# Leaf sweeps of a 64-node eigensolver: four small operations leave VectorE, three of them for ScalarE, and the order changes

## The reference, cut to what matters

```
def _L0_gnn_ref(features, A, W1, b1, W2, b2):
    deg = jnp.sum(A, axis=0) + jnp.sum(A, axis=1) - jnp.diagonal(A)
    d_inv_sqrt = jnp.where(deg > 0, jax.lax.rsqrt(deg), 0.0)
    L_norm = d_inv_sqrt[:, None] * (jnp.diag(deg) - A) * d_inv_sqrt[None, :]
    _, U = jnp.linalg.eigh(L_norm)
    agg = jnp.einsum('mn,bnd->bmd', U.T, features)
    h = jax.nn.relu(agg @ W1 + b1)
    return jnp.einsum('nm,bmd->bnd', U, h @ W2 + b2)
x = _layernorm(x + _L0_gnn_ref(x, adj, ...))   # layer 0: needs the eigenvectors
x = _layernorm(x + _L1_gnn_ref(x, adj, ...))   # layer 1: graph products, four LSTMs
x = _layernorm(x + _L2_gnn_ref(x, adj, ...))   # layer 2: products with batch norms
x = _layernorm(x + _L3_gnn_ref(x, adj, adj, ...))   # layer 3: masked attention
```

## Time and profile before

| what | value |
| --- | --- |
| median of 3 runs | 2172.83 us (2171.48 to 2173.25) |
| the profiled execution's own time | 2171.96 us |
| its span, first to last instruction | 2170.2 us |
| busy in the span: PE, PEld | 1808.6 us (83%), 1524.7 us (70%) |
| busy in the span: DVE, ACT, POOL | 1457.8 us (67%), 868.0 us (40%), 653.2 us (30%) |
| instructions | 31902 |

### The profile page before, as it was taken

The page is one execution under the profiler, slowest core; times in us unless marked ns, Lnnn a source line. Parts: engine busy times, 40 slices in busy tenths (PEclk is TensorE's granted clock), DMA queues, the critical chain, the costliest instruction groups (busy, mean ns, idle before and its releaser), DMA issues. The chain is left out here.

```text
span 2170.2 us, 31902 instructions
## 1 busy us (share of the span) xinstructions
PE 1808.6 (83%) x9508; PEld 1524.7 (70%) x9508; DVE 1457.8 (67%) x5806; ACT 868.0 (40%) x1784; POOL 653.2 (30%) x1040
## 2 busy tenths in 40 slices
PE   3454333326999999999999999999999998979997
PEld 2333333314988888888899999888887886857774
DVE  7999999985778555445444444444444777858886
ACT  2333222201344466333333333232332656646664
POOL 0001344402233466333323332413341113521111
PEclk9999766656999999999999999999999999989999
DMA  6000000000111000000000000000010412200111
GB/s 189 2 2 1 1 1 1 1 1 20 59 49 40 20 19 15 10 10 10 5 11 10 10 10 0 20 1 0 0 39 20 165 59 71 97 30 30 40 40 49
DMA packets 44689, 62.70 MB, mean 29 GB/s; under 512 B 13969, under 2 KB 33297, under 8 KB 44433
## 3 DMA queue, kind: packets, MB, share of 16 engines
q1 hardware_dynamic: 43968, 61.08, 8.3%
q10 hardware_dynamic: 592, 0.17, 0.0%
HBM read 36.08 MB, written 25.17 MB: 28 GB/s over the span
## 5 line engine op out<-in xcount | busy, mean ns | idle before, releaser
L2272 ACT ACTIVATE l_gates<-ps,biases 128x512 f32<-128x512 f32 (+1 forms) x504 | 288.9, 635 | 490.6 <-remote 476.2
L2143 PE MATMUL ps<-l_nodes_in,l_even 128*128 128x512 f32 x1392 | 321.4, 391 | 2.6 <-DVE x L1562 1.9
L2143 PEld LDWEIGHTS ps<-l_nodes_in,l_even 128*128 128x128 f32 x1392 | 260.9, 188 | 59.0 <-DVE x L1562 2.7
L2143 PE MATMUL ps<-l_nodes_in,kept 128*128 128x336 f32 (+1 forms) x1280 | 298.0, 350 | 1.9 <-ACT l_gates L2272 1.8
L2369 DVE TENSOR_TENSOR l_gates<-l_gates 128x512 f32<-128x512 f32 (+1 forms) x72 | 50.2, 697 | 343.3 <-ACT l_gates L2272 343.3
L2059 POOL CAST l_nodes_in<-big 128x512 fp32r (+3 forms) x142 | 100.3, 735 | 548.1 <-remote 520.0
L2143 PEld LDWEIGHTS ps<-l_nodes_in,kept 128*128 128x128 f32 x1280 | 229.4, 188 | 27.3 <-issue 4.3
L2143 PE MATMUL ps<-l_state,l_even 128*128 128x512 f32 x960 | 223.3, 392 | 0.0
L2143 PEld LDWEIGHTS ps<-l_state,l_even 128*128 128x128 f32 x960 | 180.4, 188 | 39.7
L2062 POOL TENSOR_TENSOR l_nodes_in<-big,l_nodes_in 128x512 fp32r<-128x512 f32 (+1 forms) x142 | 200.5, 1433 | 5.7
L995 PE MATMUL ps<-w,sw_xT 128*128 128x128 f32 x256 | 60.5, 431 | 129.6 <-ACT sw_xT L859 129.6
(11 more groups left out here) (561 smaller groups left out, 3909.7 us busy)
## 6 DMA issues: line engine op xcount, KB each, us to landing
x<-in_x SPq DMA_DIRECT2D x4, 2048.0 KB, 16.8
residual<-s_x SPq DMA_DIRECT2D x16, 512.0 KB, 2.6
x<-residual SPq DMA_DIRECT2D x16, 512.0 KB, 7.8
normed<-l_raw SPq DMA_DIRECT2D x16, 512.0 KB, 2.6
x<-normed SPq DMA_DIRECT2D x16, 512.0 KB, 3.2
out<-a_y SPq DMA_DIRECT2D x16, 512.0 KB, 2.8
l_raw<-in_L_gnn_W SPq DMA_DIRECT2D x16, 256.0 KB, 2.8
l_raw<-in_L_gnn_W SPq DMA_DIRECT2D x4, 512.0 KB, 3.6
```

What stands on the lines that cost most here:

```text
L2143: return pe.matmul(ps[:, 4 * j + gate, 0:n], weight[w_part][:, at:at + 128].bitcast(F32R), src[:, part, k, 0:n].bitcast(F32R), start=start ...
L2272: act.activation(gates[:, j, gate, 0:n], ps[:, 4 * j + gate, 0:n], ACT.Tanh if gate == G else ACT.Sigmoid, bias=bias[:, gate * KD + j:gate ...
```

## The change

On VectorE, `H2`, `floor` and `p2` go, and `ppn` and `ppx` are replaced by one product `pr` = pp x rY, from which `GX` and `G` are taken by a factor each. ScalarE gets `H2` and `p2` as squares and `floor` as 1 - act_k; the root of `mx` gets a bias of TINY, since `floor` is now exactly zero where it was TINY. The order changes: `s4` stands behind `sum`, ahead of `act_k`; `zp` ahead of `C3`; `pp` ahead of `N2`; `up` ahead of `G`; `down` directly ahead of `d`. On GpSimd, `shm` moves from ahead of `q` to behind `eby`, ahead of `cs2`. One cell is set more at the start, and there are five more semaphores.

```diff
                 after("d")
-                tt(SH[turn % 2][:, 2, :], d[:, 0:n1], d[:, 1:L], ALU.subtract).then_inc(chain[0], mark("H"))
+                tt(SH[turn % 2][:, 2, :], d[:, 0:n1], d[:, 1:L], ALU.subtract).then_inc(h_ready, 1)
                 after("dd")
                 stt(E["thr"], E["dd"], -1.0, E["dd"], ALU.mult, ALU.max).then_inc(chain[0], mark("thr"))
-                after("H")
-                tt(E["H2"], SH[turn % 2][:, 2, :], SH[turn % 2][:, 2, :], ALU.mult).then_inc(chain[0], mark("H2"))
                 after("thr", "ee")
                 tt(E["ns"], E["thr"], E["ee"], ALU.is_lt).then_inc(chain[0], mark("ns"))
-                after("H2", "ee")
-                stt(E["s4"], E["ee"], 4.0, E["H2"], ALU.mult, ALU.add).then_inc(s4_ready, 1)
...
                 tt(SH[turn % 2][:, 1, :], d[:, 0:n1], d[:, 1:L], ALU.add).then_inc(sum_ready, 1)
+                after("ee")
+                reach(h2_ready, turn)
+                stt(E["s4"], E["ee"], 4.0, E["H2"], ALU.mult, ALU.add).then_inc(s4_ready, 1)
                 after("pre")
                 scan(act_k[:, ::-1], V["pre"][:, 1:L][:, ::-1], E["ns"][:, ::-1], 0.0, ALU.max,
                      ALU.mult).then_inc(act_ready, 1)
...
-                after("T3a", "T3b")
-                tt(C3[:, :, :, 8:8 + L], T[:, 0, :, :, :], T[:, 1, :, :, :], ALU.add).then_inc(chain[0], mark("C3"))
                 if before:
                     reach(cz_ready, before)
                     scan(V["zp"], CS[:, 1, 0:L], CZ[:, 0, 0:L], 0.0, ALU.mult, ALU.add).then_inc(zp_ready, 1)
+                after("T3a", "T3b")
+                tt(C3[:, :, :, 8:8 + L], T[:, 0, :, :, :], T[:, 1, :, :, :], ALU.add).then_inc(chain[0], mark("C3"))
...
-                tt(Pp[:, 1:L + 1], T4[:, 0, :], T4[:, 1, :], ALU.add).then_inc(chain[0], mark("P"))
-                reach(act_ready, turn)
-                ts(floor[:, 0, :], act_k, 0.0, TINY, ALU.is_equal, ALU.max).then_inc(chain[0], mark("floor"))
-                after("P")
-                tt(squares[:, 0, :], Pp[:, 1:L + 1], Pp[:, 1:L + 1], ALU.mult).then_inc(chain[0], mark("p2"))
-                after("P")
+                tt(Pp[:, 1:L + 1], T4[:, 0, :], T4[:, 1, :], ALU.add).then_inc(p_ready, 1)
+                reach(p_ready, turn)
                 ts(sg[:, :], Pp[:, :], 0.0, 0.5, ALU.is_ge, ALU.subtract).then_inc(sg_ready, 1)
+                reach(p_ready, turn)
+                tt(V["pp"], Pp[:, 1:L + 1], Pp[:, 0:L], ALU.mult).then_inc(chain[0], mark("pp"))
                 reach(eb_ready, turn)
-                after("p2")
+                reach(p2_ready, turn)
                 scan(V["N2"], V["eb"], squares[:, 0, :], 1.0, ALU.mult, ALU.add).then_inc(chain[0], mark("N2"))
-                after("P")
-                tt(V["pp"], Pp[:, 1:L + 1], Pp[:, 0:L], ALU.mult).then_inc(chain[0], mark("pp"))
                 after("N2")
                 ts(Yp[:, 1:L + 1], V["N2"], TINY, None, ALU.max).then_inc(y_ready, 1)
-                after("pp")
-                tt(V["ppn"], V["pp"], V["node"], ALU.mult).then_inc(chain[0], mark("ppn"))
-                after("pp")
-                tt(E["ppx"], V["pp"][:, 1:L], act_k, ALU.mult).then_inc(chain[0], mark("ppx"))
...
                 reach(ry_ready, turn)
-                after("ppx")
-                tt(E["GX"], E["ppx"], V["rY"][:, 1:L], ALU.mult).then_inc(chain[0], mark("GX"))
+                after("pp")
+                tt(V["pr"], V["pp"], V["rY"], ALU.mult).then_inc(chain[0], mark("pr"))
...
+                after("pr")
+                tt(E["GX"], V["pr"][:, 1:L], act_k, ALU.mult).then_inc(chain[0], mark("GX"))
                 reach(ry_ready, turn)
-                after("ppn")
-                tt(V["G"], V["ppn"], V["rY"], ALU.mult).then_inc(chain[0], mark("G"))
+                tt(E["up"], Yp[:, 2:L + 1], V["rY"][:, 1:L], ALU.mult).then_inc(chain[0], mark("up"))
+                after("pr")
+                tt(V["G"], V["pr"], V["node"], ALU.mult).then_inc(chain[0], mark("G"))
...
                 reach(cs2_ready, turn)
-                after("floor")
+                reach(floor_ready, turn)
                 tt(mx[:, :, :], cs2[:, :, :], floor[:, :, :], ALU.max).then_inc(mx_ready, 1)
...
                 act.wait_ge(mx_ready, turn)
-                act.activation(sq[:, :, :], mx[:, :, :], ACT.Sqrt).then_inc(sq_ready, 1)
+                act.activation(sq[:, :, :], mx[:, :, :], ACT.Sqrt, bias=tiny).then_inc(sq_ready, 1)
...
+                act.wait_ge(h_ready, turn)
+                act.activation(E["H2"], SH[turn % 2][:, 2, :], ACT.Square).then_inc(h2_ready, 1)
                 act.wait_ge(s4_ready, turn)
                 act.activation(E["R"], E["s4"], ACT.Sqrt).then_inc(r_ready, 1)
+                act.wait_ge(act_ready, turn)
+                act.activation(floor[:, 0, :], act_k, ACT.Identity, bias=t["ones"][0:N, 0:1],
+                               scale=-1.0).then_inc(floor_ready, 1)
...
+                act.wait_ge(p_ready, turn)
+                act.activation(squares[:, 0, :], Pp[:, 1:L + 1], ACT.Square).then_inc(p2_ready, 1)
...
-                reach(tst_ready, turn)
-                reach(sum_ready, turn)
-                tt(shm[:, :, :], SH[turn % 2][:, :, :], tst[turn % 2][:, None, :].to_broadcast([N, 3, n1]),
-                   ALU.mult).then_inc(shm_ready, 1)
...
                 tt(squares[:, 1, 0:n1], E["eb"], Yp[:, 0:n1], ALU.mult).then_inc(eby_ready, 1)
+                reach(tst_ready, turn)
+                reach(sum_ready, turn)
+                reach(h_ready, turn)
+                tt(shm[:, :, :], SH[turn % 2][:, :, :], tst[turn % 2][:, None, :].to_broadcast([N, 3, n1]),
+                   ALU.mult).then_inc(shm_ready, 1)
```

More of the change, by code:

```diff
@@ L519, in sweep_leaves @@
     names = ("ee", "es", "H2", "s4", "R", "dd", "thr", "ns", "pre", "hs", "hsR", "nv", "node", "eb", "dm1", "dm", "dnn", "ad1",
-             "dxx", "ndx", "pp", "N2", "rY", "ppn", "ppx", "GX", "G", "x1", "tst", "nm", "eem", "eY", "up", "down",
+             "dxx", "ndx", "pp", "N2", "rY", "pr", "GX", "G", "x1", "tst", "nm", "eem", "eY", "up", "down",
              "q", "xx", "junk", "zp", "q1", "zero", "flip")
@@ L535, in sweep_leaves @@
     CS, CZ = sb("CS", 2, L + 1), sb("CZ", 2, L + 1)
-    one = sb("one", 2)
-    nsig, active = one[:, 0:1], one[:, 1:2]
+    one = sb("one", 3)
+    nsig, active, tiny = one[:, 0:1], one[:, 1:2], one[:, 2:3]
     flag = ctx.enter_context(nc.sbuf_tensor("sw_count", [1, 1], mybir.dt.int32))
@@ L548, in sweep_leaves @@
         "ry_ready", "rn_ready", "s4_ready", "sg_ready", "sgs_ready", "sha_ready", "shm_ready", "sq_ready",
-        "sum_ready", "ta_ready", "tst_ready", "w_ready", "xx_ready", "z_ready", "zp_ready")
+        "sum_ready", "h_ready", "h2_ready", "p_ready", "p2_ready", "floor_ready", "ta_ready", "tst_ready", "w_ready", "xx_ready", "z_ready", "zp_ready")
     (
@@ L552, in sweep_leaves @@
      eb_ready, eby_ready, es_ready, mx_ready, neb_ready, q_ready, q1_ready, ry_ready, rn_ready, s4_ready, sg_ready,
-     sgs_ready, sha_ready, shm_ready, sq_ready, sum_ready, ta_ready, tst_ready, w_ready, xx_ready, z_ready, zp_ready) = every = [sem(s) for s in signals]
+     sgs_ready, sha_ready, shm_ready, sq_ready, sum_ready, h_ready, h2_ready, p_ready, p2_ready, floor_ready, ta_ready, tst_ready, w_ready, xx_ready, z_ready, zp_ready) = every = [sem(s) for s in signals]
     act_met, pool_met, act_go, pool_go, begun_ready, pool_done, active_ready, total_ready, flag_ready, flag_used = (
@@ L596, in begin @@
                                  (V["pre"], 1.0), (V["zero"], 0.0), (V["ee"], 0.0), (SA[:, :, :], 0.0),
-                                 (SH[0][:, 0, :], 1.0), (SH[1][:, 0, :], 1.0), (floor[:, 1, :], TINY), (sgn[:, 0, :], 0.25), (CS[:, 0, :], 1.0),
+                                 (SH[0][:, 0, :], 1.0), (SH[1][:, 0, :], 1.0), (floor[:, 1, :], TINY), (tiny, TINY), (sgn[:, 0, :], 0.25), (CS[:, 0, :], 1.0),
                                  (CS[:, 1, :], 0.0), (CZ[:, :, :], 0.0), (Pp[:, 0:1], 1.0), (Yp[:, 0:1], 1.0),
@@ L743, in sweep @@
                 stt(sgn[:, 1, :], E["q"], -1.0, E["es"], ALU.mult, ALU.mult).then_inc(sgs_ready, 1)
+                after("pr")
+                tt(E["GX"], V["pr"][:, 1:L], act_k, ALU.mult).then_inc(chain[0], mark("GX"))
                 reach(ry_ready, turn)
-                after("ppn")
-                tt(V["G"], V["ppn"], V["rY"], ALU.mult).then_inc(chain[0], mark("G"))
+                tt(E["up"], Yp[:, 2:L + 1], V["rY"][:, 1:L], ALU.mult).then_inc(chain[0], mark("up"))
+                after("pr")
+                tt(V["G"], V["pr"], V["node"], ALU.mult).then_inc(chain[0], mark("G"))
                 after("GX", "ndx")
                 tt(V["x1"], V["GX"], V["ndx"], ALU.add).then_inc(chain[0], mark("x1"))
-                reach(ry_ready, turn)
-                tt(E["up"], Yp[:, 2:L + 1], V["rY"][:, 1:L], ALU.mult).then_inc(chain[0], mark("up"))
                 reach(ry_ready, turn)
```

## The result

The changed kernel takes 2177.68 us (median of 19 runs, 2175.85 to 2180.28) against 2172.83 us before (19 runs): a ratio of 1.0022, 95% interval 1.0015 to 1.0029. It is slower by 4.85 us. The profiled execution spans 2175.9 us.

A forecast was written before the change was run, and what follows sets the result against it. The sweeps' stage was taken as bound by VectorE's stream, costed by its chain of dependences; the terms sum to +0.12 us a sweep, x 32 = 3.8, with 0.1 once 3.9, hence 2176.8 us; range 2164 to 2183.

The forecast's parts named there:

- Head, +0.05: `dd` to `hsR`: chain to `pre` not shortened, `s4` pushes `act_k` and the root later; +0.05 us a sweep.
- `T3a` to `C3`, -0.07: Middle of the sweep: `T3a` shorter once `shm` no longer runs beside it; -0.07 us a sweep.
- Minors to `N2`, +0.03: `Pp` to `N2`: the trip to ScalarE for the square outweighs two removed operations; +0.03 us a sweep.
- `N2` to `rY`, -0.09: `N2` to `rY`: a bare chain once `pp`, `ppn` and `ppx` leave it; -0.09 us a sweep.
- `rY` to `d`, +0.18: Tail: `pr` adds a start behind `rY`, and `shm` adds collisions with GpSimd; +0.18 us a sweep.
- `d` to `dd`, +0.02: `d` to the next sweep's `dd`: `mx` gets a second wait, met long before; +0.02 us a sweep.
- Rival A: VectorE's stream in the sweeps is bound by operation count: four fewer give -12.8 us, 2160.0; chance 0.12.
- Rival B: Second wait on `p2` costs 0.03, `shm` falls beside `eY` or `xx`: -0.6 us, 2172; chance 0.14.
- Rival C: `shm` starts just ahead of `pr` and blocks it, `pr` taking 0.31: +0.25 a sweep, 2180.9; chance 0.18.

The follow-up runs named there:

- e1: Kernel before with only `floor` moved to ScalarE, one operation fewer on VectorE: 2172.8 us, ratio 0.9998.
- e5: Kernel before with only `ppn` and `ppx` replaced by `pr` = pp x rY: 2170.64 us, ratio 0.9994.
- e9: Kernel before with only the head changed, `H2` a square on ScalarE and `s4` behind `sum`: 2172.11 us, ratio 1.0002.
- e10: Kernel before with only GpSimd's `shm` moved behind `eby`, ahead of `cs2`: 2172.66 us, ratio 0.9999.
- e2: Changed kernel with `p2` put back on VectorE right behind `Pp`: 2177.8 us, ratio to before 1.0023.
- e3: Changed kernel with the two waits ahead of `N2` swapped, p2_ready first: 2177.16 us, ratio to before 1.002.
- e6: Changed kernel with `shm` back in its old place on GpSimd, ahead of `q`: 2177.14 us, ratio to before 1.0021.
- e8: Kernel before with the sweeps' four wait pairs turned, plus two more in the tridiagonal stage (`b`, `mixed`): 2155.23 us, ratio 0.992.
- e4: Kernel before with wait order turned, late one first, ahead of `hsR`, `nv`, `C1a` and `N2`: 2164.68 us, ratio 0.9962.
- e7: Changed kernel with the waits ahead of `hsR`, `nv`, `C1a` and `N2` turned: 2174.93 us, ratio to before 1.0012.

## Why the prediction was right, point by point

The forecast was +0.12 us a sweep and 2176.8 us; measured were 2177.68 and, by the median distance from sweep to sweep, 6.73 to 6.85, +0.12. The mean distance rose by 0.14, so some 0.02 of it lies in single longer sweeps whose cause the runs don't show. In time, +3.9 us were forecast and +4.85 measured.

In medians the parts add up: from sweep to sweep +0.01 in e1, +0.02 in e5, +0.05 in e9, nothing in e10, and the 0.04 that e2 takes back, are the 0.12. By the last column of the table the same five make only 2.1 of the 4.4 us. The rest is single longer sweeps. Their number goes with the kernel: the kernel before and e1 have three that are some 0.25 us above the median, e5 and e9 none, and the changed kernel, e3 and e6 four at the same places, 0.22 to 0.35 above it. So some 0.6 of the 4.4 us come from them, and why the change brings more of them stays open.

- *Head, +0.05.* Measured +0.05 (0.81 + 0.35 to 0.85 + 0.36), and +0.04 alone in e9. The chain from `dd` to `pre` did not shorten, and `act_k` was pushed by `s4`, as forecast.
- *`T3a` to `C3`, -0.07.* Measured -0.07. That `shm` was the cause is shown by e10 and e6.
- *Minors to `N2`, +0.03.* Measured +0.05: the square took 0.22, not 0.20, and the second wait cost its 0.10. The term was mis-sized by 0.02. With the square back on VectorE (e2) it is 0.47 again, as before.
- *`N2` to `rY`, -0.09.* Measured -0.09, and -0.09 in e5.
- *`rY` to `d`, +0.18.* Measured +0.17, of which e5 gives 0.09 to `pr` and e10 0.06 to `shm`. The forecast had these at 0.11 and 0.07. Inside the term two errors cancelled, which was luck. Three collisions were forecast, 0.21 in sum; only `pr` (0.23) and `G` (0.25) are recorded long, and the starts behind them come 0.15 later in sum. But `pr` starts 0.30 behind `rY` and not 0.27, and the stretch without its collisions takes 0.98, where the forecast had 0.94.
- *`d` to `dd`, +0.02.* Measured +0.01 in the median. The second wait of `mx`, met long before, costs about nothing. The bias of the root was not 0.1 us once: the root takes 0.32 instead of 0.23 in every sweep, but nothing waited for it (`rn` starts 1.5 us behind its end).

That the sum is right to 0.01 us is luck in part as well: the 0.02 too little for the minors is made up by 0.01 too much in each of the last two terms.

Rival A, counting, is excluded by e1 and e9 one operation at a time, and e2 shows an operation added that makes the sweeps shorter. The rule of "VectorE: DVE Perf Modes" (Rules for kernel authors) in the Trainium skill, to minimize the operation count and not the semaphores, did not hold for this chain: one operation fewer gained nothing (ratios 0.9998 in e1 and 1.0002 in e9), and the order of waits alone, with every operation in place, gained 0.8% (e8). The same page's section "The DRAIN you can't avoid", which the prediction sets against the starts 0.09 apart, also says that a next operation that is not held starts earlier, so those starts need not speak against the Trainium skill. The count did pay in one place, `N2` to `rY`, where more operations stood than the hole could take (-0.09 in e5).

Rival B asked for `N2`'s wait at 0.03 and for `shm` beside `eY` or `xx`, which it took to be free. e3 had the first, and its 0.07 went into the longer `Yp`. e10 had the second, and it is not free: `xx` grows by 0.08, and `GX` behind it starts that much later. Rival C's condition was met, for `shm` does start ahead of `pr`, but its price did not occur. `pr` took 0.23 and not 0.31, because `shm` was 0.28 long and had started 0.08 before, not 0.05. The Trainium skill's page "SBUF — State Buffer" (Who interferes with whom) describes an exclusive port pair, the later of the two blocked to the other's end. e10 agrees: `xx` ends at 326.01, 0.02 behind `shm`.

## What to carry to other kernels

In a stream of tiny dependent operations, first mark the holes: an operation that stands in one is free (`floor` in e1), and taking it out gains nothing. Handing it to another engine can cost: the square on ScalarE is a trip of 0.03 + 0.22 + 0.03 to 0.10 us. Where an operation has two waits, issue the one that is met last first. Look which one that is in the profile, and look again after every reordering, since a late wait in the second place cost 0.04 to 0.07 here at each of the six operations. Where such a gain brings the next operation beside one of GpSimd it can be lost again, as in e3.

## What the hardware showed that I had not expected

- The place of a wait. With the late wait last, an operation starts 0.10 us behind its producer's recorded end; with it first, 0.03 to 0.04 (`N2` in the earlier trace rows and in e4, and behind ScalarE in e3; `hsR` in e7 the other way round). In the tridiagonal stage it is 0.11 to 0.05 for `b` and 0.13 to 0.06 for `mixed` (e8). I had read the 0.10 in the trace of before as a constant of the chain. It was worth 17 us of 2172 in six places.
- A collision moved was a collision kept. Moving GpSimd's `shm` (0.26 to 0.33 us) gave -0.07 in one place and +0.06 in the other in e10, +0.07 and -0.08 in e6, and e3's 0.07 went into a `Yp` beside `q1`. It is not a law: in e4 `rY` to `d` became 0.03 shorter. But a gain in one link of such a chain counts only once the neighbouring GpSimd operations have been followed as well.
